# A layer kernel on one core: the static buffers moved by 32 to 800 bytes, every instruction left in its place

## The reference

```python
# layer 0
normed = _layernorm(hidden, g1, b1)
q, k, v = normed @ Wq + bq, normed @ Wk + bk, normed @ Wv + bv     # then split in heads
logits = q k^T / sqrt(Hd) + (2.0 * adj - 1.0)
weights = softmax(logits) * (0.25 + 0.75 * adj)
weights = weights / maximum(weights.sum(-1), 1e-6)
hidden = hidden + (weights v) @ Wo + bo
h2 = _layernorm(hidden, g2, b2)
x = hidden + gelu(h2 @ Wf1 + bf1) @ Wf2 + bf2                      # Wf1 256x1024, Wf2 1024x256
# layer 1
e = leaky_relu(s[:, :, :, None] + t[:, :, None, :], 0.2) + adj     # s, t from layer_norm(x) @ W1
attn = softmax(e) h + x                                            # 8 heads
out = (the same with W2 and one head) + attn
```

## Time and profile before

| | |
|---|---|
| median of three runs | 1115.22 us (1115.18 to 1118.21) |
| the profiled execution | 1118.75 us, its span 1116.9 us |
| PE busy | 1060.2 us, 95% of the span |
| PE weight loads busy | 927.2 us, 83% |
| DVE, ACT, POOL busy | 800.2, 714.8, 398.1 us |
| mean granted clock of TensorE | 0.985 of full speed |
| the chain that ended last | PE 79%, DVE 8%, issue 5%, POOL 3%, ACT 2% |

### The profile page before, as it was taken

How to read it: one execution, slowest core, us unless ns; L and a number is a source line. 1 busy time by engine, 2 the same in 40 slices (tenths; PEclk the granted TensorE clock), 3 DMA queues, 4 the chain that set the end, 5 groups by cost and what they waited for, 6 DMA issues and landing times.

```text
span 1116.9 us, 39179 instructions
## 1 busy us (share of the span) xinstructions
PE 1060.2 (95%) x15924; PEld 927.2 (83%) x15924; DVE 800.2 (72%) x1935; ACT 714.8 (64%) x1718; POOL 398.1 (36%) x628
## 2 busy tenths in 40 slices
PE   6999999999999989999999999999899999969997
PEld 5888888888888868899889988998878888868886
DVE  4677777777777768856555656545779889849996
ACT  2777677777677755544554455546678888847774
POOL 3531121211211113411131113212368878775562
PEclk9999999999999999999999999999989999989998
DMA  9211112211110011100110011010000000002212
GB/s 245 49 40 41 40 40 51 67 40 40 41 40 21 3 34 36 29 19 22 30 27 19 21 29 29 20 38 11 12 22 27 19 26 21 5 2 77 70 64 96
DMA packets 82476, 43.67 MB, mean 39 GB/s; under 512 B 42912, under 2 KB 77984, under 8 KB 82336
## 3 DMA queue, kind: packets, MB, share of 16 engines
q1 hardware_dynamic: 78016, 41.44, 13.6%
q10 hardware_dynamic: 4320, 0.28, 0.3%
HBM read 21.25 MB, written 12.58 MB: 30 GB/s over the span
## 4 chain that ended last, share of the span: by engine, by line
PE 79%; DVE 8%; issue 5%; POOL 3%; ACT 2%; SPq 1%; DMA 1%; DVEq 0%; POOLq 0%; ACTq 0%
PE BK L1334 8%; PE BK L1336 8%; PE BK L1335 8%; PE BK L1463 6%; PE BK L1550 5%; PE BK L1552 5%; PE BK L1551 5%; PE BK L1437 5%; PE BK L1449 4%; PE BK L1430 3%; PE BK L1350 3%; PE BK L1359 3%; PE BK L1597 3%; PE BK L1351 2%; PE BK L1352 2%
## 5 line engine op out<-in xcount | busy, mean ns | idle before, releaser
L1182 ACT ACTIVATE gf<-BK,bcol 128x512 f32<-128x512 f32 x128 | 88.4, 690 | 168.9 <-PE BK L1336 152.4
L955 POOL TENSOR_TENSOR ve<-mv,eps_l 128x4 f32<-128x4 f32 x64 | 18.2, 284 | 460.8 <-DVE mv L316 428.5
L1098 ACT ACTIVATE e_sb<-BK,nmx 128x128 f32<-128x128 f32 x512 | 142.4, 408 | 28.3 <-DVE nmx L503 28.3
L599 DVE TENSOR_TENSOR gl<-gf,gh 128x512 fp32r<-128x512 f32 x128 | 97.6, 765 | 73.8 <-ACT gh L1183 73.2
L1550 PE MATMUL BK<-wf_hi,gh 128*128 128x256 f32 x512 | 145.3, 284 | 1.4 <-DVE gl L599 1.4
L1552 PE MATMUL BK<-wf_lo,gh 128*128 128x256 f32 x512 | 145.0, 283 | 0.0
L1551 PE MATMUL BK<-wf_hi,gl 128*128 128x256 f32 x512 | 144.5, 282 | 0.0
L509 DVE TENSOR_TENSOR pt_sb<-BK,ft 128x512 f32<-128x512 f32 x128 | 85.2, 686 | 60.6 <-PE BK L1437 58.8
L1118 ACT ACTIVATE xn<-x_all,neg_mr,rstd 128x256 f32<-128x256 f32 (+1 forms) x188 | 103.8, 611 | 4.7 <-POOL neg_mr L964 4.4
L1334 PE MATMUL BK<-xh,wf_hi 128*128 128x512 f32 x256 | 101.2, 395 | 1.0 <-DVE x_all L525 0.5
L1336 PE MATMUL BK<-xh,wf_lo 128*128 128x512 f32 x256 | 101.0, 394 | 0.0
(11 more groups left out here) (206 smaller groups left out, 2822.6 us busy)
## 6 DMA issues: line engine op xcount, KB each, us to landing
x_all<-in_x_dram SPq DMA_DIRECT2D x16, 512.0 KB, 4.8
out_dram<-y SPq DMA_DIRECT2D x16, 512.0 KB, 2.8
xn<-tb_ln SPq DMA_DIRECT2D x240, 32.0 KB, 1.9
adj_in<-in_adj_dram SPq DMA_DIRECT2D x64, 64.0 KB, 3.7
adj_kept<-adj_tr SPq DMA_DIRECT2D x16, 256.0 KB, 2.3
adj_in<-adj_kept SPq DMA_DIRECT2D x16, 256.0 KB, 2.7
s_wf<-in_L_gnn_Wf_dram SPq DMA_DIRECT2D x2, 1024.0 KB, 6.8
s_w<-in_L_gnn_W_dram SPq DMA_DIRECT2D x2, 256.0 KB, 2.9
```

The costliest lines, as they stand in the source:

```text
L599: dve.tensor_tensor(gl[:, f, :], gf[f % 2][:], gh[:, f, :].bitcast(F32), ALU.subtract).then_inc(b_gl, 1)
L1098: e = act.activation(e_sb[:, j, :], LE[:, r, q, :], ACT.Exp, bias=nmx[:, j:j + 1], scale=1.0)
L1182: act.activation(gf[f % 2][:], BK[:, f % 4, :], ACT.Gelu, bias=bcol[:, 6 + f:7 + f])
```

## The change

The pads of `sb` are gone, and the places in overlays are rounded up to 32 bytes and not to 64. The order of instructions is the same on every engine, row by row; only line numbers are 2 lower, and the addresses of operands differ.

```diff
         def sb(name, shape, dt=F32):
-            if (nc.sbuf_base + 31) // 32 % 2:
-                ctx.enter_context(nc.sbuf_tensor(f"pad_{name}", [P, 8], F32))
             return ctx.enter_context(nc.sbuf_tensor(name, shape, dt))
...
-        base_of_x = (nc.sbuf_base + 63) // 64 * 64
+        base_of_x = (nc.sbuf_base + 31) // 32 * 32
...
-        at_wq = (nc.sbuf_base + 63) // 64 * 64
+        at_wq = (nc.sbuf_base + 31) // 32 * 32
...
-                at_wf1 = (nc.sbuf_base + 63) // 64 * 64
+                at_wf1 = (nc.sbuf_base + 31) // 32 * 32
...
-        base_of_region = (nc.sbuf_base + 63) // 64 * 64
+        base_of_region = (nc.sbuf_base + 31) // 32 * 32
...
-                at[0] += (n + 63) // 64 * 64
+                at[0] += (n + 31) // 32 * 32
```

## The result

The changed kernel took 1103.45 us (median of four runs, 1102.11 to 1106.47) against 1115.24 us (four runs, 1115.18 to 1118.21). The ratio is 0.9889, with a 95% interval of 0.9867 to 0.9910. I had forecast 1115.3 us, no change, with 1110 as the lower end.

The account below looks back on a forecast made before the run. The prediction took PE streaming its operands as the bound in A and B, with PE and DVE alternating in C and D. Its terms, 0 + 0 + 0 + 0 + 0.1 us, on 1115.22 gave 1115.3 us, range 1110 to 1121.5.

Parts of the forecast that it names:

- What changes for it is the distance: Stage B: moving minus stationary operand modulo 512 goes from 384 to 320 on wf1, 128 to 192 on wf2.
- The trace has both new distances elsewhere ... I take 0 for all of it: Stage B streams: intervals already seen at distances 320 and 192 match the old ones, so the effect was priced at 0.
- The w2 rows: Even chunks of stage D: w2_lo streaming while xh loads, distance 192, 120 ns, taken as the sample for wf2.
- The wst1 sample: Odd chunks' xh2 streaming over wst1, distance 320: 4 intervals of 232.5 ns, taken as the sample for wf1.
- The bounds on wf2: Stage B, 1536 matmuls: two phases 1.4 ns apart at the same addresses, giving -2.2 to +2.2 us.
- The ceiling: Stage B: excess over 2.4 GHz streaming, the most an address could change, 34 us.
- The rival that came true: Streamed operand and load conflict, new distance eases it: a fifth of B's excess, -6.8 us, with A 1106 us; chance 0.11.
- The share of stage A: Matmuls on wq, wk and wv: forecast 0, bounds -1.5 to +1.5 us; the easier-conflict rival put it at -2.5 us.
- Starts 32 bytes off: Stages C and D, 496 matmuls with operands 32 off a multiple of 64: 0, bounds -5.0 to +5.0 us.
- My slower rival: Stages C and D: starts off a multiple of 64 slow PE's weight loads, +5.0 us, 1120.3 us; chance 0.12.
- Other engines and DMAs: DVE and ACT 0, bounds -1 to +1 us; tb_ln transfers +0.1 us; output transfers 0.
- The clock: Stages C and D: half-clock stretches may come or go, 1.7 or 3.4 us each; chance 0.08, half each side.

Follow-up runs that it names:

- e4: Changed kernel with 128 bytes more before the weights, so weights and activations both moved and their distance stayed 192; 1101.93 us.
- e2: Changed kernel with 128 bytes more before the weights and 384 before xn, so only the weights moved, back to their old place; 1115.29 us.
- e3: Changed kernel with 192 bytes more before xn, so only activations and region moved, back to their old place; 1113.39 us.
- e1b: Kernel before, multiples of 64 kept, with pads giving weights, activations and region the changed kernel's places; 1105.77 us against 1115.55, ratio 0.9904.
- e6: Changed kernel with xn and all behind it moved by 448 bytes, weights minus activations 256; 1113.3 us.
- e9: Changed kernel with gl and all behind it, gf included, moved 64 bytes on in stage B's overlay; 1114.12 us.
- e13: Changed kernel with gf alone moved 64 bytes on in stage B; whole time not given, chunk of stage B 21.89 us.
- e14: Changed kernel with gl moved 64 bytes on and gf back at its place modulo 256; 1113.04 us.

## Why the prediction was wrong

**What bounds the kernel: right.** In A and B the time is PE's streams. It is because of this that 6 ns on one kind of matmul became 9 us: 1536 x (119.5 - 113.7) = 8.9 us, and 768 x (232.5 - 229.2) = 2.5 us, 11.4 us together for the whole of B. The measured 10.3 us is a little less, since the first two chunks and the last wait for other engines too, and parts of them run in the slower rhythm.

**"What changes for it is the distance": right, with the wrong modulus.** I named the distance between the streamed and the loaded operand as the only thing that changes. The runs confirm it (e4 against e2 and e3), with a period of 256 bytes instead of 512.

**"The trace has both new distances elsewhere ... I take 0 for all of it": this is the step that failed.** I put this term at nothing, with bounds of -2.2 us for wf2 and -1.9 us for wf1, and by the intervals it measured -8.9 and -2.5 us. The price came from two samples, of 4 and 3 intervals, and neither was a settled run at the new distance.

The w2 rows were no run at that distance at all. Only w2_lo lay at 192; its matmuls alternate with those of w2_hi at 128, so two in a row never streamed at 192. The wst1 sample did lie at the new distance, but it is the start of a run of 6 behind other work. The changed kernel's first wf1 run starts behind other work too, and once past its first interval it has 229, 237, 231 and 232 ns, 232.3 on average, and only then about 229. In the changed kernel's own wf2 chunk above it is likewise the first five intervals that are 118 ns. So the samples held a start and a mixture, and I read them as settled values. Such short runs don't follow the distance: the even chunks' wst1 runs had 234.1 ns before and 230.5 after on their second to fifth intervals, at a distance of 0 modulo 256 in both. Length alone is not the rule: runs of 12 on w1 in stage C do reach 114 ns, and the 17 intervals of 117.6 ns in the first chunk do not. The prediction took one steady value for each distance, and there are several.

The bounds on wf2 were drawn from two rhythms at the old distance, and so said nothing about the new one. The ceiling that I worked out, 34 us in stage B, was the honest bound: with no settled run at the new distance, it should have gone into the range. The change took 11 of these 34 us.

**The rival that came true** is the second one: an excess of 13 and 19 ns that the new distance eases. I priced a fifth of the excess in B at -6.8 us and gave it 0.11. In B it was a third: the 12.8 ns on wf2 became 7.0, the 19.2 ns on wf1 15.9. The argument that I put against it was the sample above. What I had put for it, that the excess changes with the phase at fixed addresses, was the better sign.

**The share of stage A: near 0 is right.** The rival's -2.5 us for A was too much; A ended 1.0 us earlier in one profile and 0.4 us in the other. Most of its projections run in pieces of 6 matmuls behind other work, as the wst1 runs do, and keep their intervals; in the few longer pieces on wv the later intervals fell from 118.7 to 114 to 116 ns.

**Starts 32 bytes off: 0 is right.** With the rule kept (e1b) the gain is the same within the intervals, 0.9904 against 0.9889. My slower rival had no ground.

**Other engines and DMAs: right in size.** The medians of DVE and ACT are unchanged, tb_ln's DMAs land in 1.9 us as before, and the wait at the start of B stands. Of the transfers that I priced, y's got slower, 2.9 us for 2.8. All 17 profiles agree on this: 2.8 us in the three kernels whose y starts at a multiple of 256 (before, e3 and e6), 2.9 us in the 14 others. Only the last of them ends the kernel, so as an estimate it costs 0.1 us, where I had priced a tenth more at 0.3 us.

The Trainium skill says that a transaction can read less than 256 bytes but has to start at a multiple of 256, so that an unaligned descriptor also fetches bytes in front of its start ("DMA: Bandwidth & Descriptors", section "How a descriptor splits into AXI transactions"). The trace agrees in direction for the transfers that read y. For those that write xn it shows nothing: 1.9 us with xn at a multiple of 256 and off one. The transfers that read adj_tr, whose start moves along with y's, take 2.3 or 2.4 us and don't follow it. So that the transactions are the cause is not shown. One transaction more, as the prediction puts it, follows for pieces of 512 bytes; the Trainium skill's own example of 96 bytes keeps a single one.

**The clock: right as noise.** Stage C differs by 4.6 us between two profiles of the same program, with 6.8 and 17.0 us at half clock within it. The first comparison of spans, 16.7 us, held about 5 us of such luck; the medians differ by 11.8.

## What to carry to other kernels

Where PE streams float32r pairs back to back, look at the interval between starts, and compare it with the columns at the granted clock. If it exceeds them by some per cent (here 6 to 12%), try other distances between the streamed and the loaded operands: here six distances modulo 256 bytes lay up to 3.4% of a chunk apart (21.89 to 22.66 us). Judge only long runs in the place where they run, and don't add up the best distance of each part: measure the whole.

When a sample is to stand for an unseen cost, it has to be as long as the thing it stands for, and made of nothing else. If none is, keep the full ceiling in the range.

## What the runs showed of the hardware that was not expected

- The interval between float32r matmuls depends on the distance of streamed and loaded operand modulo 256 bytes (given as weights minus activations): 113.7 to 119.9 ns for 256 columns, 227.2 to 233.3 ns for 512, exactly repeated by kernels 256 bytes apart (chunk periods of 22.42, 22.51, 22.66 and 21.89 us, each twice). Single places 32 bytes apart differ as well.
- Of the six distances tried, the best for one kind of stream is not the best for the other: 192 for wf2 (256 columns, weights streaming), 0 for wf1 (512 columns, activations streaming). Whether the length or the exchanged roles make the difference is not shown.
- At the same distance there can be several rhythms: 118.6 and 120.0 ns at 128, 113.6 and 117.6 to 117.8 ns at 192, 229 and 233.3 ns for wf1. A chunk in the steady part of stage B takes its own after about five matmuls; after a wait it can be another one.
- y's transfers of 512 KB to the output land 0.1 us sooner (2.8 and 2.9 us) when y starts at a multiple of 256 bytes.
- What meets inside the chip was not shown. That two reads of PE meet is my reading of e4, e9, e13 and e14, and nothing else that touches gl is left in the last run of stage B; a run without any load beside the stream, which would prove it, was not made. How the rhythms arise, and why the two kinds of stream prefer different distances, stays open too.
